# A two-layer metaformer step on one Trainium2 core: all five engine orders rewritten, FFN pixels turned by DMA, moments on VectorE

## The chip, the cores and the metric

One NeuronCore of a Trainium2 chip. The metric is the device time of one launch in microseconds, as the median of several executions. The kernel drives five engines with their own instruction streams: TensorE (PE), VectorE (DVE), ScalarE (ACT), GpSimd (POOL) and SyncE (SP, which only issues DMAs). They meet in semaphores alone.

## What is computed

`x` has the shape (16, 96, 96, 96): 16 images, 96 channels, 96 x 96 pixels. Two layers follow one another; every token is one pixel with its 96 channels.

```
# layer 0
x = x + conv0(_ln_c(x))                 # patches of 3x3, see below
t = t + ffn(_ln_t(t))                   # 96 -> 384 -> relu -> 96, operands rounded to e5m2, sums to fp16
# conv0, for each 3x3 patch (9 pixels):
y       = patches . w_mask / (x_norm * w_norm)       # cosine with 512 vectors, 9 pixels each
idx     = argmax over 512 x 9 ; max_ch, max_col = idx // 9, idx % 9
inp     = [max_act * max_sim + w_mask[max_ch] * (1 - max_sim), y[max_ch, :]]
out     = 1x1 conv of l2(relu(l1(tanh(i2(leaky_relu(i1(inp)))))))
# layer 1
x = x + n / (2 + 1e-4 * box5x5(sum_c n^2)) ** 0.75   # n = _ln_c(x)
t = t + ffn(_ln_t(t))
```

## The kernel before

**Tiles.** A tile is 128 patches of 9 pixels (`J` = 9), so 128 partitions x 9 x 96 values; an image has 8 tiles (`SLOTS`), the input 128 (`NT`). `x_tok` holds a tile with tokens on the partitions, `x_chan` with channels on them.

**Steps.** One software-pipelined loop, `steps(body)`, runs on each engine over k from -4 on. In step k each stage works on another tile, by the offsets in `PARTS`: `fs` (k+4, statistics of the input), `f1` (k+3, scores), `f2` (k+2, the picked vector), `f3` (k+1, the MLP and conv), `back` (k, hidden part of the first FFN `ffn0`), `tail` (k-1, its output), `root2` (k-2, sums for LRN), `columns` and `pre` (k-10, k-11, LRN applied and layer-1 normalisation), `rear` (k-12, hidden part of `ffn1`) and `rtail` (k-13, its output and the store). Within a step, the order of the work is written out by hand in the `body` of each engine, and each engine does its instructions in that order. Once per image come `window_parts` and `window_sums` (step 1 of 8: the 5 x 5 box as 15 shift matmuls) and `lrn_columns` (step 2 of 8: the polynomial and a root, some 25 instructions on VectorE).

**Stages that the change touches.**
- `score` (L383) multiplies a pixel with the 512 vectors, one fp32 matmul into one of two banks, and waits in `score_taken` for VectorE's `score_max` (L742) of two scores before. `win_scores` (L401) puts the picked pixel's scores into the same banks; the score behind it waits for `vidx_ready` from `win_vector` (L783).
- `select` (L750) on VectorE finds the best pixel of a patch; three instructions with an accumulator (L771 to L776) pick its mean, its reciprocal deviation and its best score. `gather_pixel` and `gather` on GpSimd fetch rows by indirect DMA; `dot_product` on GpSimd multiplies them with the nine pixels.
- `mlp_input` (L791) on VectorE builds `inp` (the last instruction is L807). The MLP goes back and forth: `mlp_turn` (L407), `mlp_in`, `mlp_mid`, `mlp_last`, `conv` on TensorE with ScalarE's copies `inpT`, `h`, `vcs`, `h1` between, and `residual1` (L810) on VectorE at its end.
- Statistics: `group_stats` (L736) runs `bn_stats` over 9 pixels for three tiles (input, `x1`, `x2`); `moments` (L947) on GpSimd turns them into means, sums of squares and arguments of roots with nine chained instructions; `pixel_roots` (L721) on VectorE takes the roots at the start of the next step (`args_ready`, then `root_ready`). GpSimd's `body` waits for `root_ready` before anything else.
- Both FFNs pass through two PSUM banks each in 14 units a tile (`UNITS`): 3 units turn the fp8 pixels (L363: transposes by matmul with an identity; ScalarE copies them to `xT`), 9 make the hidden values (L370, 384 columns each), 2 the output (L378). `fill` on TensorE and `take` on ScalarE alternate over `filled` and `taken`; VectorE adds the bias, applies relu and rounds to e5m2 (`hidden`, L820: L825 three times, L833 once).
- `ffn_output` (L989) on GpSimd adds bias and residual in two passes per FFN.
- SyncE loads `xt` and `xc` of tile `fs` (`load_tokens`, `load_pixels`), then stores the tile `rtail`.

## Time and profile before

| | before |
|---|---|
| median of 3 runs | 3559.91 us (3558.04 to 3561.16) |
| the profiled execution | 3554.84 us, its span 3553.0 us |
| busy PE / DVE / ACT / POOL | 3011.0 / 2778.1 / 2832.7 / 2566.0 us |
| mean granted TensorE clock | 0.958 of full |
| HBM read / written | 134.72 / 57.02 MB |

A row of the profile's page or of the trace gives times in us from the start of the span, durations in us (ns where marked), and the line of the kernel. A row with xN stands for N instructions of a kind that follow one another. An instruction's duration includes its passage through the engine's pipeline, so the next one of the same engine may start before it ends; a busy time is the union of such durations. In square brackets stands how long the engine was idle ahead of the instruction, and for whom.

### The profile page before, as it was taken

To read this page: it belongs to the slowest core of one execution; us is meant where nothing else is said; L and a number is where in the kernel's file an instruction comes from. 1 tells how busy PE (TensorE), PEld (TensorE's weight loads), DVE (VectorE), ACT (ScalarE), POOL (GpSimd) and SP (SyncE) were. 2 spreads that over 40 slices of the span, in tenths; PEclk is the share of its full clock that TensorE was granted. 3 is DMA by queue.
4 is the path that set the end of the run, shared out by engine and by line. 5 is a ranking of instruction groups with operands and counts; after the bars stand their busy time and mean duration, and the time that the engine had idled before them with its cause. 6 is when DMAs were issued, how large, how long until landed. Compare 5 with 4: busy or idle time off the path is not lost. (4 is left out here: it accounts for less than half of the span.)

```text
span 3553.0 us, 62660 instructions
## 1 busy us (share of the span) xinstructions
PE 3011.0 (85%) x18190; PEld 1688.2 (48%) x18190; DVE 2778.1 (78%) x10043; ACT 2832.7 (80%) x7303; POOL 2566.0 (72%) x3993
## 2 busy tenths in 40 slices
PE   5888888888888888888888888888888888888755
PEld 2444454454545445445544545454444555445432
DVE  6777888888888888888888888888888888888631
ACT  0444788888888888888888888888878888888977
POOL 2455787777778777777877777787777778777753
PEclk9999999999999999999999999999999999999855
DMA  3111121211112121111212111121212112121000
GB/s 88 38 45 47 45 63 52 65 54 57 61 57 62 52 67 51 57 61 56 62 52 67 52 58 60 57 62 52 66 51 64 55 57 62 52 66 42 24 31 35
DMA packets 64607, 195.78 MB, mean 55 GB/s; under 512 B 11394, under 2 KB 14732, under 8 KB 64268
## 3 DMA queue, kind: packets, MB, share of 16 engines
q1 hardware_dynamic: 54028, 172.89, 15.1%
q0 software_dynamic: 10240, 18.89, 2.1%
q8 instruction: 150, 2.46, 0.3%
q14 instruction: 189, 1.55, 0.1%
HBM read 134.72 MB, written 57.02 MB: 54 GB/s over the span
## 5 line engine op out<-in xcount | busy, mean ns | idle before, releaser
L527 ACT ACTIVATE ffn_hid<-banks 128x384 f16<-128x384 f32 x2304 | 1026.8, 487 | 260.0 <-PE banks L370 236.7
L393 PE MATMUL banks<-wcT,xc 128*128 128x512 f32 x2304 | 1187.8, 618 | 50.2 <-DVE mx L745 43.4
L745 DVE TENSOR_REDUCE mx<-banks 128x1 f32<-128x512 f32 x1152 | 781.4, 687 | 428.8 <-PE banks L393 427.6
L370 PE MATMUL banks<-ffn_xT,w1q 128*128 128x384 bf16 x2304 | 668.8, 343 | 177.3 <-ACT ffn_hid L527 138.0
L994 POOL TENSOR_TENSOR ffn_f<-ffn_y,b2q 128x864 f16<-128x864 f16 x256 | 465.3, 1818 | 288.3 <-DVE nb L731 209.7
L370 PEld LDWEIGHTS banks<-ffn_xT,w1q 128*128 128x128 bf16 x2304 | 226.1, 98 | 775.8 <-ACT ffn_hid L527 589.4
L393 PEld LDWEIGHTS banks<-wcT,xc 128*128 128x128 f32 x2304 | 414.5, 196 | 282.8 <-issue 140.8
L825 DVE TENSOR_SCALAR ffn_hid<-ffn_hid,b1q 128x1152 f16<-128x1152 f16 x768 | 405.8, 551 | 139.0 <-ACT ffn_hid L527 138.6
L996 POOL TENSOR_TENSOR x<-x,ffn_f 128x864 f32<-128x864 f32 x256 | 466.6, 1823 | 20.1
L560 ACT ACTIVATE ffn_x<-x,cols 128x96 fp8e5<-128x96 f32 x1152 | 461.3, 456 | 0.0
L560 ACT ACTIVATE ffn_x<-x,nb,roots 128x96 fp8e5<-128x96 f32 x1152 | 425.1, 456 | 0.0
L738 DVE BATCH_NORM_STATS2 st<-x 128x6 f32<-128x96 f32 x2304 | 406.0, 245 | 13.1 <-POOL x L996 13.1
L984 POOL TENSOR_TENSOR prod_dot<-xt,wrow 128x864 f32<-128x864 f32 x128 | 263.3, 2057 | 195.4 <-DMA wrow<-vector_table,vidx 195.4
L437 PE MATMUL banks<-wc,h 128*128 128x480 f32 (+1 forms) x1024 | 393.8, 528 | 0.0
L527 ACT ACTIVATE ffn_xT<-banks 96x384 bf16<-96x384 f32 x768 | 345.0, 484 | 57.0 <-PE banks L363 37.1
L378 PEld LDWEIGHTS banks<-w2q,ffn_hid 128*128 128x128 f16 x6912 | 335.0, 100 | 116.6 <-issue 115.1
L527 ACT ACTIVATE ffn_y<-banks 128x480 f16<-128x480 f32 (+1 forms) x512 | 256.8, 531 | 161.3 <-PE banks L378 144.7
L378 PE MATMUL banks<-w2q,ffn_hid 128*128 128x96 bf16 x6912 | 351.3, 210 | 37.1 <-DVE ffn_hid L833 37.1
L363 PE MATMUL banks<-ident_b,ffn_x 128*96 128x128 bf16 x2304 | 227.6, 227 | 146.9 <-ACT ffn_xT L527 118.8
L363 PEld LDWEIGHTS banks<-ident_b,ffn_x 128*96 128x96 fp8e5 x2304 | 175.8, 125 | 257.1 <-ACT ffn_xT L527 157.2
L573 ACT ACTIVATE x<-x,cols 128x96 f32<-128x96 f32 x640 | 293.5, 461 | 0.2 <-POOL cols L1004 0.2
L833 DVE TENSOR_SCALAR ffn_hid<-ffn_hid 128x3456 uint16<-128x3456 uint16 x256 | 270.5, 1057 | 4.0
(153 smaller groups left out, 4178.6 us busy)
## 6 DMA issues: line engine op xcount, KB each, us to landing
xt<-x_tok_in SPq DMA_DIRECT2D x128, 432.0 KB, 3.2
xc<-x_chan_in SPq DMA_DIRECT2D x128, 432.0 KB, 3.6
out_tok<-x SPq DMA_DIRECT2D x128, 432.0 KB
win<-x_tok_in,xrow POOLq DMA_INDIRECT x128, 2.6
wrow<-vector_table,vidx POOLq DMA_INDIRECT x128, 2.9
shift<-shift_in SPq DMA_DIRECT2D x1, 960.0 KB
vector_table<-wtab SPq DMA_DIRECT2D x1, 384.0 KB, 2.9
w1raw<-w_in SPq DMA_DIRECT2D x1, 288.0 KB
```

Of the source, the lines that this page charges most:

```text
L363: last = pe.matmul(bank[0:C, i * P:(i + 1) * P], ffn.x8[:, u * G + i, :], ident_b[:, :], start=True, stop=True)
L370: last = pe.matmul(bank[:, 0:GW], w1q[:, ffn.layer, c * P:(c + 1) * P], ffn.xT[:, g * GW:(g + 1) * GW], start=True, stop=True)
L378: last = pe.matmul(bank[:, (j - j0) * C:(j - j0 + 1) * C], ffn.hid[:, c, j * P:(j + 1) * P], w2q[:, ffn.layer, c, :], start=(c == 0), stop ...
L393: last = pe.matmul(ps_score[score_bank(j)], xc[p][:, j, :], wcT[:, :], start=True, stop=True)
L437: last = pe.matmul(bank[:, 0:(j1 - j0) * C], h1[:, q, :], wc[:, q, j0 * C:j1 * C], start=(q == 0), stop=(q == 1))
L527: return nc.scalar.activation(dst, src, ACT.Copy)
L560: last = nc.scalar.activation(ffn.x8[:, j, :], x[:, j, :], ACT.Identity, bias=bias_c[:, j:j + 1], scale=scale_c[:, j:j + 1], saturate=False)
L738: last = nc.vector.bn_stats(st3[:, which, j, :], src[:, j, :])
L745: nc.vector.tensor_reduce(mx[p][:, j:j + 1], ps_score[score_bank(j)], AX.X, ALU.max).then_inc(score_taken, 1)
L825: nc.vector.tensor_scalar(ffn.hid[:, c, :], ffn.hid[:, c, :], b1q[:, ffn.layer, c:c + 1], 0.0, ALU.add, ALU.max).then_inc(ffn.rounded, 1)
L994: tt(ffn.f[:, :, :], ffn.y[:, :, :], b2, ALU.add).then_inc(ffn.f_ready, 1)
L996: tt(dst, x, ffn.f[:, :, :], ALU.add).then_inc(ready, 1)
```

## The change

Only the order and place of work change, and two steps of how it is done:

- The fp8 pixels of each FFN are no longer turned on TensorE. ScalarE writes them in pairs (`x8` [P, 5, 128, 2]: two pixels' bytes side by side), SyncE issues one `dma_start_transpose` for each FFN and tile over 5 x 128 two-byte elements of 128 partitions, and the hidden matmuls read `xT` with a step of two bytes, in pieces of 512, 512 and 128 columns. `UNITS` becomes 11.
- `moments` moves from GpSimd to VectorE: seven instructions, woven with `select` at the end of the step. The three accumulating picks become one product and one reduction over `pix`, in which twice the mean, sum of squares and roots lie together; a third `mix` instruction halves the mean.
- `keep_root2` becomes one copy, `tile_columns` one; the squares for LRN are made once per image (two instructions more in `window_parts`).
- GpSimd no longer waits for `root_ready` at the head of its step; its order is bias of `ffn1`, bias and sum of `ffn0`, LRN rest, `gather`, `keep_root2`, `window_parts`, `dot_product`, `tile_columns`, `gather_pixel`, and the sum of `ffn1` last.
- SyncE turns both FFNs' pixels, then loads for the next step, then stores.
- The bodies of TensorE, ScalarE and VectorE are ordered anew, as below.

```diff
-UNITS = G + HC * G + 2
+COLUMNS = [(0, 512), (512, 1024), (1024, J * P)]
+UNITS = HC * G + 2
@@ sync
+            def turn(ffn, tile):
+                sp.wait_ge(ffn.x8_ready, tile + 1)
+                wait_past(sp, ffn.filled, tile * UNITS - 2)
+                sp.dma_start_transpose(ffn.xT[:, :, :], ffn.x8[:].rearrange("p a c t -> p (a c t)").bitcast(F16)
+                                       ).then_inc(ffn.turned, 16)
             def body(k):
+                if k.back is not None:
+                    turn(ffn0, k.back)
+                if k.pre is not None:
+                    turn(ffn1, k.pre)
+                load(Step(k.k + 1))
                 if k.rtail is not None:
                     sp.wait_ge(x4_ready, k.rtail + 1)
                     sp.dma_start(out[k.rtail], x4[k.q][:]).then_inc(x4_stored[k.q], 16)
@@ tensor, fill
-                    if u < G:
...
-                        for i in range(J // G):
-                            last = pe.matmul(bank[0:C, i * P:(i + 1) * P], ffn.x8[:, u * G + i, :],
-                                             ident_b[:, :], start=True, stop=True)
+                    if u < HC * G:
+                        c, g = divmod(u, G)
                         if u == 0:
-                            pe.wait_ge(ffn.x8_ready, tile + 1)
+                            pe.wait_ge(ffn.turned, (tile + 1) * 16)
+                        c0, c1 = COLUMNS[g]
+                        pairs = ffn.xT[:, c0 // (2 * P):(c1 + P) // (2 * P), :].bitcast(F8).rearrange(
+                            "p a (x t) -> p a t x", t=2)
...
+                        last = pe.matmul(bank[:, 0:c1 - c0], w1q[:, ffn.layer, c * P:(c + 1) * P], pairs,
+                                         start=True, stop=True)
@@ tensor, body
                 scores(0, 2)
-                if k.tail is not None:
-                    fill(ffn0, k.tail, G + HC * G, 2)
+                hidden_units(ffn1, k.rear, 0, 2)
+                out_units(ffn0, k.tail, k.tail_p, 0)
+                out_units(ffn0, k.tail, k.tail_p, 1)
+                hidden_units(ffn1, k.rear, 2, 2)
+                scores(2, 3)
                 if k.f3 is not None:
                     mlp_turn(k.f3)
-                if k.rear is not None:
-                    fill(ffn1, k.rear, 0, G)
+                hidden_units(ffn1, k.rear, 4, 1)
+                if k.f2 is not None:
+                    win_turn(k.f2, k.q)
...
                 if k.f3 is not None:
                     mlp_in(k.f3)
+                hidden_units(ffn1, k.rear, 5, 1)
+                scores(3, WIN_TURN)
                 if k.f2 is not None:
+                    win_scores(k.f1, k.f2)
...
                     mlp_mid(k.f3)
+                scores(WIN_TURN, 5)
+                hidden_units(ffn1, k.rear, 6, 2)
+                scores(5, 6)
                 if k.f3 is not None:
                     mlp_last(k.f3)
+                scores(6, 7)
+                hidden_units(ffn1, k.rear, 8, 1)
                 if k.f3 is not None:
                     conv(k.f3)
-                if k.back is not None:
-                    fill(ffn0, k.back, 0, G)
                 hidden_units(ffn0, k.back, 0, 2)
                 scores(7, 8)
                 hidden_units(ffn0, k.back, 2, 2)
+                scores(8, J)
                 window_sums(k, 0, 5)
-                scores(8, J)
                 hidden_units(ffn0, k.back, 4, 2)
                 window_sums(k, 5, 10)
+                out_units(ffn1, k.rear, k.rear_p, 0)
+                out_units(ffn1, k.rear, k.rear_p, 1)
                 hidden_units(ffn0, k.back, 6, 3)
@@ scalar, body (norm0: nine pixels of ffn0, behind root_ready; norm1: of ffn1)
+                take_hidden(ffn1, k.rear, 5, 1)
+                norm0(k, 0, 3)
+                lrn_pixels(k, 4, XA)
+                norm0(k, 3, 5)
                 ... vcs ...
+                norm0(k, 5, J)
+                take_hidden(ffn1, k.rear, 6, 1)
                 ... h1 ...
+                take_hidden(ffn1, k.rear, 7, 2)
+                norm1(k, 0, XA)
+                norm1(k, XA, XA + 1)
+                take_hidden(ffn0, k.back, 0, 2)
+                norm1(k, XA + 1, XA + 2)
+                take_hidden(ffn0, k.back, 2, 2)
+                norm1(k, XA + 2, J)
+                take_hidden(ffn0, k.back, 4, 2)
+                take_out(ffn1, k.rear, k.rear_p)
+                take_hidden(ffn0, k.back, 6, 3)
@@ vector
+            def moments(tile, p):
+                dve.wait_ge(stats_ready, tile + 1)
+                wait_past(dve, root_ready, tile)
+                wait_past(dve, kept, tile - 6)
...
@@ vector, body
+                    mlp_input(k.f3, k.p, roots_of, lambda: scores(0, 1))
+                run(roots_of, 3)
+                scores(1, 2)
+                run(roots_of, 2)
+                scores(2, 3)
+                run(roots_of)
+                scores(3, WIN_TURN, factors, 2)
+                relu(ffn1, k.rear, 0)
+                    last = group_stats(1, xt[:, k.fs & XT - 1], 0, 6, factors)
+                    win_vector(k.f2, k.q, factors)
+                    last = group_stats(1, xt[:, k.fs & XT - 1], 6, J, factors)
+                scores(WIN_TURN, 5, factors, 2)
+                relu(ffn1, k.rear, 1)
+                    last = group_stats(2, x2[:, k.tail & RING - 1], 0, 6, factors)
+                scores(5, 7, factors, 2)
+                relu(ffn1, k.rear, 2)
+                    last = group_stats(2, x2[:, k.tail & RING - 1], 6, J, factors)
+                run(factors)
+                round_up(ffn1, k.rear)
                     residual1(k.f3, k.q)
                 scores(7, 8)
+                    last = group_stats(0, x1[k.q], 0, J, iter(()))
                 scores(8, J)
+                for c in range(HC):
+                    for _ in range(2):
+                        run(moments_of, 1)
+                        run(select_of, 1)
...
+                    relu(ffn0, k.back, c)
+                round_up(ffn0, k.back)
@@ gpsimd, body
-                if k.moments is not None:
-                    pool.wait_ge(root_ready, k.moments + 1)
+                if k.rtail is not None:
+                    ffn_bias(ffn1, k.rtail, x4_ready)
                 if k.tail is not None:
+                    ffn_bias(ffn0, k.tail, x2_ready)
                     ffn_output(ffn0, k.tail, x1[k.q][:, :, :], x2[:, k.tail & RING - 1], x2_ready)
...
-                if k.stats is not None:
-                    moments(k.stats, k.q)
                 if k.f1 is not None:
                     gather_pixel(k.f1, k.p)
+                if k.rtail is not None:
+                    pool.wait_ge(x4_stored[k.q], landed(k.rtail, k.q))
+                    ffn_output(ffn1, k.rtail, x3[:, k.rtail3], x4[k.q][:, :, :], x4_ready)
```

## Rows read from the trace of the kernel before

**Rows 1.** The profile's page, head: busy us, share of the span, instructions
```profile
span 3553.0 us, 62660 instructions
PE 3011.0 (85%) x18190; PEld 1688.2 (48%) x18190; DVE 2778.1 (78%) x10043; ACT 2832.7 (80%) x7303; POOL 2566.0 (72%) x3993
```

**Rows 2.** One line's instructions (L803): ns min/median/max, first and last start us
```profile
L803 DVE TENSOR_SCALAR wnorm<-win,wmean,mix x128: 318/329/422, 64.3 to 3326.9; 128x96 f32<-128x96 f32 x128
```

**Rows 3.** Stretches between store issues, and the end: from:to, length, busy by engine
```profile
1759.84:1786.80 26.96, 24.39 (x166) 15.53 (x167) 20.41 (x76) 21.66 (x57) 23.57 (x44) 1.00 0.18 56
1786.80:1816.99 30.19, 24.55 (x141) 13.12 (x139) 27.10 (x97) 22.55 (x59) 19.49 (x30) 0.94 0.15 50
1816.99:1841.86 24.87, 22.18 (x138) 12.39 (x138) 20.59 (x76) 22.04 (x58) 19.46 (x30) 1.00 0.19 60
3326.86:3553.00 226.14, 127.75 (x795) 71.93 (x791) 71.19 (x163) 170.71 (x434) 112.11 (x179) 0.57 0.08 30
```
(The engines stand in the order PE, PE's weight loads, DVE, ACT, POOL; then TensorE's granted clock, the DMA engines' busy share and GB/s.)

**Rows 4.** Timeline of VectorE in a plain step: start us, us, instruction [idle before]
```profile
1836.17 0.69 DVE L745 TENSOR_REDUCE mx<-banks 128x1 f32<-128x512 f32 x1 [0.62 <-PE banks L393]
...
1849.97 0.69 DVE L745 TENSOR_REDUCE mx<-banks 128x1 f32<-128x512 f32 x1 [1.17 <-PE banks L393]
...
1855.24 0.19 DVE L765 TENSOR_TENSOR xrow<-jidx,row_base 128x1 uint32<-128x1 uint32 x1
1855.36 0.16 DVE L767 TENSOR_TENSOR pick<-iota,jidx 128x9 f32<-128x9 f32 x1
1855.55 0.20 DVE L771 SCALAR_TENSOR_TENSOR junk<-pick,mom 128x9 f32<-128x9 f32 x1
...
1855.87 0.59 DVE L798 TENSOR_REDUCE dots<-half_dot 128x9 f32<-128x432 f32 x1
...
1857.22 0.31 DVE L807 SCALAR_TENSOR_TENSOR inp<-wrow,mix,wnorm 128x96 f32<-128x96 f32 x1
...
1858.14 0.20 DVE L718 SCALAR_TENSOR_TENSOR roots<-rtmp,roots 128x36 f32<-128x36 f32 x1
1858.37 0.20 DVE L708 SCALAR_TENSOR_TENSOR rtmp<-roots 128x36 f32<-128x36 f32 x1
```

**Rows 5.** Timeline of TensorE in the same step
```profile
1832.73 0.32 PE L410 MATMUL banks<-ident,inp 128*106 128x128 f32 x1 [0.39 <-DVE inp L807]
1832.88 0.50 PE L363 MATMUL banks<-ident_b,ffn_x 128*96 128x128 bf16 x6
...
1834.01 0.85 PE L415 MATMUL banks<-inpT,wi 106*96 106x128 f32 x6
...
1845.17 1.88 PE L393 MATMUL banks<-wcT,xc 128*128 128x512 f32 x4
1846.89 0.50 PE L363 MATMUL banks<-ident_b,ffn_x 128*96 128x128 bf16 x6
...
1857.59 0.32 PE L410 MATMUL banks<-ident,inp 128*106 128x128 f32 x1 [0.38 <-DVE inp L807]
```

**Rows 6.** Waits from 1500 to 2400 us: who for whom, us, times, longest
```profile
DVE mx L745 <- PE banks L393: 110.7, 205, 1.3
...
PE banks L363 <- ACT ffn_xT L527: 33.1, 70, 1.0
```

**Rows 7.** Timeline of GpSimd in the same step: first and last of `moments`
```profile
1852.19 0.49 POOL L955 TENSOR_TENSOR mtmp<-st 128x27 f32<-128x27 f32 x2 [1.04 <-DVE st L738]
...
1856.26 0.25 POOL L962 TENSOR_TENSOR args<-var,eps 128x27 f32<-128x27 f32 x1
```

**Rows 8.** Timeline of ScalarE in the same step: three copies of turned pixels
```profile
1833.28 1.42 ACT L527 ACTIVATE ffn_xT<-banks 96x384 bf16<-96x384 f32 x3
```

**Rows 9.** The page's DMA issues: KB each, median us from issue to landing
```profile
xt<-x_tok_in SPq DMA_DIRECT2D x128, 432.0 KB, 3.2
...
wrow<-vector_table,vidx POOLq DMA_INDIRECT x128, 2.9
```

More of the change, by code:

```diff
@@ L20 @@
 from contextlib import ExitStack
+from itertools import chain
 import numpy as np
@@ L158, in build @@
         pow_half = sb("pow_half", [P, V // P])
-        half, c24, inv_c = (sb(n, [P, 3, J]) for n in ("half", "quarter_c", "inverse_c"))
         eps = sb("eps", [P, 3, J])
@@ L590, in take_hidden, with take_out @@
                     if tile is not None:
-                        take(ffn, tile, G + first, units)
-                if k.tail is not None:
-                    take(ffn0, k.tail, G + HC * G, 2)
-                lrn_pixels(k, 0, 1)
+                        take(ffn, tile, k.back_p if ffn is ffn0 else k.rear_p, first, units)
+                def take_out(ffn, tile, parity):
+                    if tile is not None:
+                        take(ffn, tile, parity, HC * G, 2)
+                take_hidden(ffn1, k.rear, 0, 1)
+                lrn_pixels(k, 0, 1)
+                take_hidden(ffn1, k.rear, 1, 1)
+                lrn_pixels(k, 1, 2)
+                take_out(ffn0, k.tail, k.tail_p)
+                take_hidden(ffn1, k.rear, 2, 2)
+                lrn_pixels(k, 2, 3)
                 if k.f3 is not None:
@@ L661, in _ @@
             nc.vector.memset(wc[:], 0.0)
-            for operand in (*xc, wcT, winT, w1q, ffn0.xT, ffn1.xT):
+            for ffn in (ffn0, ffn1):
+                nc.vector.memset(ffn.x8[:].rearrange("p a c t -> p (a c t)").bitcast(U16), 0)
+            for operand in (*xc, wcT, winT, w1q):
                 last = nc.vector.memset(operand[C:P], 0.0)
@@ L889, in body, with scores @@
             def body(k):
-                between = pixel_roots(k) if k.moments is not None else iter(())
-                def scores(j0, j1, links=0):
+                roots_of = pixel_roots(k) if k.moments is not None else iter(())
+                factors = lrn_columns(k.lrn, k.pre) if k.lrn is not None else iter(())
+                last = None
+                def scores(j0, j1, between=iter(()), links=0):
                     for j in range(j0, j1):
@@ L927, in body @@
                 scores(8, J)
-                between = select(k.f1, k.p) if k.f1 is not None else iter(())
-                if k.back is not None:
-                    hidden(ffn0, k.back, between)
-                run(between)
+                select_of = select(k.f1, k.p) if k.f1 is not None else iter(())
+                moments_of = moments(k.stats, k.q) if k.stats is not None else iter(())
+                for c in range(HC):
+                    for _ in range(2):
+                        run(moments_of, 1)
+                        run(select_of, 1)
+                    if c == HC - 1:
+                        run(moments_of)
+                        run(select_of)
+                    relu(ffn0, k.back, c)
+                round_up(ffn0, k.back)
             steps(body)
```

322 lines of the change are left out of this document (141 added, 181 removed).

## The prediction

> **What bounds the kernel now.** The head of the page comes first: TensorE is busy 85% of the span, ScalarE 80%, VectorE 78%, GpSimd 72% [rows 1]. None is full, so the order of work between them counts. The step is regular: the `wnorm` instruction of line 803 runs 128 times from 64.3 to 3326.9 us, so a step takes 25.69 us on average [rows 2]. Cut from store issue to store issue there are three kinds: 24.87 us for a plain step, 26.96 us for the one with the window sums, 30.19 us for the one with the LRN polynomial, each of the last two once in eight [rows 3]. Those eight make 6 x 24.87 + 26.96 + 30.19 = 206.4 us. By busy time the plain step has 22.18 us of TensorE, 20.59 of VectorE, 22.04 of ScalarE and 19.46 of GpSimd; the LRN step has 27.10 of VectorE [rows 3].
>
> The loop that closes the step is read from two timelines. TensorE starts `mlp_turn` (L410) right behind VectorE's `inp` (L807) at 1832.73, works through both transposes, the MLP and seven scores, and gives score 7, for which VectorE has waited 1.17 us at 1849.97 [rows 4, 5]. From there VectorE works without a wait to L807 at 1857.22, and TensorE, idle since its last projection, starts the next L410 at 1857.59. That is 17.2 us on TensorE and 7.6 us on VectorE. In this half TensorE runs nine fp8 transposes twice and is held by ScalarE's copies of them. The waits agree: over 35 steps the transposes wait 33.1 us for `ffn_xT`, and VectorE 110.7 us for scores [rows 6]. GpSimd closes no loop: its last moments instruction, at 1856.26, is done before VectorE comes to the root chain [rows 7].
>
> **Part 1, pixels turned by DMA.** It removes 18 transposes from TensorE and 6 copies from ScalarE in each step. On TensorE the first block runs from 1832.88 to the next work at 1834.01, 1.1 us, and the second, from 1846.89 on, is its like with 0.2 us of waits more, so 2.4 us in all [rows 5]; on ScalarE 6 copies, 3 of them in 1.42 us, give 2.7 us [rows 8]. The hidden matmuls keep 1152 columns in 9 pieces (512, 512, 128 in place of 3 x 384), so I cost that at zero, between -0.3 and +0.5 us a step; the cover is two scores or pixels beside each pair. That the moving operand now steps over two bytes has no row here: from nothing to 2.9 us of TensorE (18 hidden matmuls of 384 columns of 0.16 us each, once more), and I take nothing: even the upper end would go into the slack that TensorE has below.
>
> The added thing is the latency of two DMAs of 160 KB a step. No row shows such a DMA. The nearest are the 432 KB token load, 3.2 us to landing, and the gathers, 2.9 us [rows 9]. I take 3.5 us, with 2.9 and 8 us as the ends. The cover for `ffn0`: its normalised pixels are ready some 9.5 us behind the start of VectorE's step, and its first hidden unit is wanted at 13.5; the loss begins at about 4.5 us of latency and grows one for one. For `ffn1` pixels end at about 16 and are wanted at 19.5 to 22, a cover of 5 us or so. The queue of SyncE carries them ahead of the next loads and behind the store of the step before. The load of tile k+5 is then issued near 16.5 us and used a step later, which hides it; the store now waits for GpSimd's last sum, and must be issued before 9.5 us of the next step, which it is by some 8 us.
>
> The Trainium skill (Advanced Engine Details and Errata, X-Bar Transpose) says that a transposing DMA on this chip is about as fast as a plain one, at 350 to 400 GB/s. By it the 160 KB would add under 0.5 us to a gather's 2.9 us, an estimate of 3.4 us, and the DMA would be hidden. No row here shows one.
>
> **Part 2, moments on VectorE.** GpSimd's chain from 1852.19 to 1856.5 goes, 4.3 us a step [rows 7], and with five copies fewer GpSimd keeps about 14.7 of its 19.46 busy us. VectorE gains seven 27-element instructions. A dependent one of 36 elements has a pitch of 0.23 us in the root chain (1858.14 to 1858.37), neighbours without a dependency 0.12 us (1855.24 to 1855.36) [rows 4]. Woven into `select` they lie between: I take 0.15 us, 1.05 us in all, ends 0.8 and 1.6. Three accumulating picks (1855.55 to the next work at 1855.87, 0.32 us) become a product and a reduce (0.35), and one more `mix` costs 0.12. The sum is +1.2 us.
>
> The Trainium skill (VectorE: DVE Perf Modes, The DRAIN you can't avoid) speaks against this part: the pipe empties behind each VectorE instruction, with or without a semaphore, so the count of instructions is what costs. This case's trace agrees for the dependent pitch of 0.23 us and not for the 0.12 us of neighbours.
>
> **Part 3, the new order.** VectorE takes score 0 inside `mlp_input`, and TensorE calls `mlp_turn` after score 2, with four hidden units and the output projection ahead of it. From L410 to score 7 I count on TensorE by start-to-start time: five scores of 0.86 (two run from 1845.17 to 1846.89 [rows 5]), 4.3; the window score 0.86; the MLP's three matmul groups 2.1; conv 2.9 (up to 1845.17); hidden units 1.2 and two turns 0.5. That makes 11.8 us against 17.2. VectorE's half grows from 7.6 to 9.4 us (moments 1.2, score 0 at 0.6). The two are 21.2 us, and four handovers of 0.2 to 0.4 us (L807 to L410 is 0.37) bring them to about 22.4: as much as VectorE's own work, below.
>
> **The step after.** VectorE now: 24.87 less its seven waits of the sample step (0.62 at 1836.17 the first, 1.17 at 1849.97 the last, 3.91 in all) is 20.96 us [rows 4]. With +1.2 it is 22.2 us, the floor of the plain step. TensorE's sum by pitch is 19.2 us (ten scores 8.6, conv 2.9, MLP and turns 2.5, hidden 2.9, projections 2.3), ScalarE's 22.04 - 2.7 = 19.3, GpSimd's 14.7. What is late next is VectorE itself, then two tight handovers: `vidx` ahead of score 5 and score 7 behind conv, each within 0.4 us by my count. I add 0.6 us for such waits: 22.8 us. The window step keeps its +2.0 (15 shift matmuls in TensorE's slack, but GpSimd's window parts also end just in time): 24.8. The LRN step is already VectorE's own, 27.10 us busy of 30.19 [rows 3]; it becomes 27.1 + 1.2 and about 1.1 of gaps, 29.4. Eight steps: 6 x 22.8 + 24.8 + 29.4 = 191.0, so 15.4 us less, times 127/8 = 245 us.
>
> **Ends.** Set-up gains some memsets and a first turn, +2 us. From 3326.86 to the end, 226 us, there are thirteen shorter steps without a score, in which ScalarE's takes, VectorE's rounding and the projection follow one another, with TensorE's mean granted clock at 0.57, so mostly at its lower level of 1.2 GHz [rows 3]. There the DMA is not covered; the transposes, their copies and one wait (some 3 us) leave and 3.5 us comes, +5 us over the last 11 steps. Sum: span 3553.0, time of the profiled run 3554.8; 3554.8 - 245 + 7 = 3317. The median is 5.1 us above the profiled run, which gives 3322; I say 3320.
>
> **Rivals.**
> (A) The forecast, VectorE-bound at 22.2 to 23.6 us: 3240 to 3430 us, 57%.
> (B) The coupling keeps some of it: in-order ScalarE has `norm0` (nine pixels behind the root chain) ahead of `vcs` and `h1`, so conv comes late, and the step settles at 24.0 us. For it: today's loop holds over 2 us of waits on TensorE though none looks long. Price 1.2 x 127 = 152 us, so about 3470 us; 21%.
> (C) Each small VectorE instruction costs its full chain pitch of 0.23 us, ten of them 2.3 in place of 1.2 us: +1.1 x 127, some 3460 us; for it the root chain's even 0.23, against it the 0.12 pairs; 8%, inside the range of B. The rule on the pipe in the Trainium skill (VectorE: DVE Perf Modes, The DRAIN you can't avoid) is this rival.
> (D) The turning DMA is late, on the other side. It decides from 4.5 us of latency, and equals today's time at about 6.6 us (24.87 - 22.8 = 2.1 above 4.5). At 8 us each step is 3.5 longer, +445 us, and the drain +50: 3815 us. For it: it moves 81 920 elements of two bytes, where the rows below 3.6 us move whole runs of one partition, and nothing bounds its rate; against it: 432 KB land in 3.2 us, nearly three times its bytes. 12%, of which 10 are above 6.6 us and slower than before.
> (E) The change does nothing for the time, because ScalarE (22.04 busy) was the real bound and only its 2.7 us count against longer takes: within 0.2% of before, 2%.
>
> **Numbers.** Measurements here can tell about 0.2% from no change. Faster: A, B, C and 2 in 100 for a late DMA below 6.6 us, 0.88; same 0.02 (E); slower 0.10. The range 3235 to 3490 holds A, B and C but for their tails; it leaves out D and some of E.
>
> **What would show it.** Plain steps of 22.8 us between stores; VectorE idle under 1 us a step; no wait of TensorE for `ffn_xT`; landing of the turned pixels at 3 to 4.5 us; GpSimd near 63% busy. The prediction is wrong if hidden matmuls wait for the DMA (D), if VectorE still waits over 1.5 us a step for scores or for conv (B), or if the moments take over 1.6 us (C).

## The result, and the profile after

| | before | after |
|---|---|---|
| median | 3558.97 us | 4008.78 us |
| ratio | 1 | 1.127 (1.1244 to 1.1288) |
| profiled execution, its span | 3554.84, 3553.0 us | 4007.11, 4005.3 us |
| VectorE, GpSimd busy | 78%, 72% | 94%, 51% |

The change makes the kernel 12.7% slower; 3320 us was forecast, within 3235 to 3490. One of the four executions of the changed kernel took 4324.45 us at a mean granted clock of 0.639 (0.893 in the profiled one) and is not in the ratio.

The head of the page of the changed kernel answers to [rows 1], the row of `wnorm` (now L870; min, median and max ns, first and last start) to [rows 2]:

```profile
span 4005.3 us, 55754 instructions
PE 2981.2 (74%) x15886; PEld 1626.2 (41%) x15886; DVE 3770.5 (94%) x10587; ACT 2459.5 (61%) x6535; POOL 2047.7 (51%) x1799
...
L870 DVE TENSOR_SCALAR wnorm<-win,mix x128: 315/317/326, 66.0 to 3802.8; 128x96 f32<-128x96 f32 x128
```

A mean step takes (3802.8 - 66.0) / 127 = 29.42 us against 25.69. Stretches of the changed kernel between store issues, as in [rows 3] (the window step, the LRN step, a plain one, and all that follows the last `wnorm`; engines in the order PE, PE's weight loads, VectorE, ScalarE, GpSimd; then granted clock, DMA share, GB/s):

```profile
1726.32:1755.66 29.34, 23.66 (x147) 15.19 (x148) 28.11 (x80) 17.54 (x47) 19.79 (x28) 0.94 0.22 62
1755.66:1788.59 32.93, 24.04 (x125) 11.79 (x123) 32.59 (x102) 21.13 (x55) 15.50 (x12) 0.95 0.19 56
1818.43:1848.25 29.82, 21.70 (x120) 12.09 (x120) 29.55 (x80) 19.04 (x51) 15.61 (x12) 0.94 0.21 62
3802.83:4005.30 202.47, 106.35 (x651) 57.40 (x649) 89.24 (x184) 147.64 (x380) 94.00 (x93) 0.57 0.15 46
```

VectorE works 29.55 of the 29.82 us of a plain step, so it is the bound, as forecast, yet with about as many instructions as before (80 against 76) it is busy 9 us longer. TensorE, ScalarE and GpSimd have all become lighter. TensorE's granted clock is lower (0.94 of full in the plain step, 1.00 in the kernel before), but that isn't the cause: VectorE waits 26 us for scores in the whole run, where it waited 428. What grew is found by grouping VectorE's instructions by line and shape (count | busy us, mean ns | idle before). First the kernel before, then the changed one; L718 became L752, L708 L742, L711 L745, L715 L749, L825 (relu) L891 and L833 (rounding) L899:

```profile
L745 DVE TENSOR_REDUCE mx<-banks 128x1 f32<-128x512 f32 x1152 | 781.4, 687 | 428.8 <-PE banks L393 427.6
L825 DVE TENSOR_SCALAR ffn_hid<-ffn_hid,b1q 128x1152 f16<-128x1152 f16 x768 | 405.8, 551 | 139.0 <-ACT ffn_hid L527 138.6
L833 DVE TENSOR_SCALAR ffn_hid<-ffn_hid 128x3456 uint16<-128x3456 uint16 x256 | 270.5, 1057 | 4.0
L711 DVE TENSOR_TENSOR rtmp<-rtmp,args 128x36 f32<-128x36 f32 x266 | 52.1, 196 | 9.1
L718 DVE SCALAR_TENSOR_TENSOR roots<-rtmp,roots 128x36 f32<-128x36 f32 x266 | 52.0, 196 | 9.1
L708 DVE SCALAR_TENSOR_TENSOR rtmp<-roots 128x36 f32<-128x36 f32 x266 | 51.4, 193 | 4.8
L715 DVE SCALAR_TENSOR_TENSOR rtmp<-rtmp 128x36 f32<-128x36 f32 x133 | 26.0, 196 | 4.5
```

```profile
L812 DVE TENSOR_REDUCE pix<-banks 128x1 f32<-128x512 f32 x1152 | 770.0, 677 | 26.3 <-PE banks L417 26.0
L891 DVE TENSOR_SCALAR ffn_hid<-ffn_hid,b1q 128x1152 f16<-128x1152 f16 x768 | 761.6, 992 | 104.0 <-ACT ffn_hid L552 104.0
L899 DVE TENSOR_SCALAR ffn_hid<-ffn_hid 128x3456 uint16<-128x3456 uint16 x256 | 483.9, 1890 | 4.8
L752 DVE SCALAR_TENSOR_TENSOR pix<-rtmp,pix 128x36 f32<-128x36 f32 x266 | 259.2, 974 | 4.8
L742 DVE SCALAR_TENSOR_TENSOR rtmp<-pix 128x36 f32<-128x36 f32 x266 | 237.2, 892 | 4.7
L745 DVE TENSOR_TENSOR rtmp<-rtmp,args 128x36 f32<-128x36 f32 x266 | 100.8, 379 | 4.8
L749 DVE SCALAR_TENSOR_TENSOR rtmp<-rtmp 128x36 f32<-128x36 f32 x133 | 56.6, 425 | 4.5
```

The score reduction, which reads PSUM, is unchanged (687 and 677 ns). Relu went from 551 to 992 ns on the same 1152 elements, rounding from 1057 to 1890, the root chain's instructions on 36 elements from some 195 to 974, 892, 379 and 425. Per step (six relus, two roundings, seven root instructions) that is 6 x 0.441 + 2 x 0.833 + 2 x (0.778 + 0.699 + 0.183) + 0.229 = 7.9 us. The forecast's floor of 22.2 and 7.9 make 30.1, and the plain step takes 29.8.

Where the time sits is seen in the timeline of a plain step of the changed kernel: VectorE and then GpSimd over the same stretches (start, duration, instruction):

```profile
1844.98 0.51 DVE L891 TENSOR_SCALAR ffn_hid<-ffn_hid,b1q 128x1152 f16<-128x1152 f16 x1
...
1845.89 2.66 DVE L891 TENSOR_SCALAR ffn_hid<-ffn_hid,b1q 128x1152 f16<-128x1152 f16 x1
1848.58 2.55 DVE L899 TENSOR_SCALAR ffn_hid<-ffn_hid 128x3456 uint16<-128x3456 uint16 x1
...
1853.39 0.20 DVE L745 TENSOR_TENSOR rtmp<-rtmp,args 128x36 f32<-128x36 f32 x1
...
1854.33 1.74 DVE L752 SCALAR_TENSOR_TENSOR pix<-rtmp,pix 128x36 f32<-128x36 f32 x1
1856.11 1.87 DVE L742 SCALAR_TENSOR_TENSOR rtmp<-pix 128x36 f32<-128x36 f32 x1
```

```profile
1845.26 1.12 POOL L1030 DMA_INDIRECT win<-x_tok_in,xrow  x1 [5.27 <-DVE xrow L832]
1846.39 1.83 POOL L1061 TENSOR_TENSOR x<-x,ffn_f 128x864 f32<-128x864 f32 x1
1848.37 1.85 POOL L1056 TENSOR_TENSOR ffn_f<-ffn_y,b2q 128x864 f16<-128x864 f16 x1
1854.21 1.81 POOL L1056 TENSOR_TENSOR ffn_f<-ffn_y,b2q 128x864 f16<-128x864 f16 x1 [3.99 <-ACT ffn_y L552]
1856.10 1.82 POOL L1061 TENSOR_TENSOR x<-x,ffn_f 128x864 f32<-128x864 f32 x1
```

One relu takes 0.51 us, its like 0.9 us later 2.66, ending 0.3 us behind GpSimd's add. A root instruction takes 0.20 us while GpSimd is idle and 1.74 and 1.87 us when GpSimd's adds of 864 elements (L1056, L1061) start just before it. In the kernel before the same adds stood here (its timeline, GpSimd first, then VectorE):

```profile
1834.44 1.82 POOL L994 TENSOR_TENSOR ffn_f<-ffn_y,b2q 128x864 f16<-128x864 f16 x1 [1.43 <-DVE nb L731]
1836.33 1.82 POOL L996 TENSOR_TENSOR x<-x,ffn_f 128x864 f32<-128x864 f32 x1
```

```profile
1834.27 1.28 DVE L745 TENSOR_REDUCE mx<-banks 128x1 f32<-128x512 f32 x2
1836.17 0.69 DVE L745 TENSOR_REDUCE mx<-banks 128x1 f32<-128x512 f32 x1 [0.62 <-PE banks L393]
1837.97 1.53 DVE L738 BATCH_NORM_STATS2 st<-xt 128x6 f32<-128x96 f32 x9
```

They fall on score reductions and statistics, at their usual durations. Over the whole run, the 465 us of L994 overlap VectorE for 234 us in L738, 166 us in L745 and some 1 us in a relu; the 472 us of L1056 overlap it for 182 us in the rounding, 28 in relu and 211 in the root chain, and the 468 us of L1061 for 222 us in relu and 225 in the root chain. GpSimd's wait for `root_ready`, which the change takes away, starts them behind the root chain (runs 1 and 2 test this).

The turned pixels are no trouble. The page's DMA issues (answers to [rows 9]; count, median us to landing) and the waits of the whole run (total, times, longest):

```profile
ffn_xT<-ffn_x SPq DMA_TRANSPOSE x256, 2.6
```

```profile
PE banks L394 <- DMA ffn_xT<-ffn_x: 18.4, 12, 1.9
```

### The profile page after: what moved, and what is told of

It reads as the page before. It is cut to its first block, busy times and chain, and to the rows that moved or that the text cites. A ratio compares the mean times of both kernels' runs of the same rounds, so it can differ in the third digit from the quotient of the medians.

```text
span 4005.3 us, 55754 instructions
## 1 busy us (share of the span) xinstructions
PE 2981.2 (74%) x15886; PEld 1626.2 (41%) x15886; DVE 3770.5 (94%) x10587; ACT 2459.5 (61%) x6535; POOL 2047.7 (51%) x1799
## 4 chain that ended last, share of the span: by engine, by line
DVE 70%; issue 13%; PE 6%; POOL 4%; ACT 3%; DMA 3%; SPq 0%; POOLq 0%; DVEq 0%
DVE ffn_hid L891 15%; DVE st L803 11%; DVE pix L812 11%; DVE pix L752 6%; DVE rtmp L742 5%; DVE ffn_hid L899 4%; DVE x L882 3%; DVE rtmp L745 2%; DVE vidx L852 2%; PE banks L417 2%; DVE dots L862 2%; DMA win<-x_tok_in,xrow 1%; ACT ffn_hid L552 1%; DVE rtmp L749 1%; PE banks L462 1%
## 5 line engine op out<-in xcount | busy, mean ns | idle before, releaser
L552 ACT ACTIVATE ffn_hid<-banks 128x512 f16<-128x512 f32 (+1 forms) x2304 | 1032.4, 490 | 382.0 <-PE banks L394 381.2
L402 PE MATMUL banks<-w2q,ffn_hid 128*128 128x96 bf16 x6912 | 447.2, 238 | 614.2 <-DVE ffn_hid L899 614.2
L891 DVE TENSOR_SCALAR ffn_hid<-ffn_hid,b1q 128x1152 f16<-128x1152 f16 x768 | 761.6, 992 | 104.0 <-ACT ffn_hid L552 104.0
L394 PE MATMUL banks<-ffn_xT,w1q 128*128 128x512 fp8e5 (+1 forms) x2304 | 688.5, 355 | 148.4 <-ACT ffn_hid L552 123.1
L812 DVE TENSOR_REDUCE pix<-banks 128x1 f32<-128x512 f32 x1152 | 770.0, 677 | 26.3 <-PE banks L417 26.0
L1056 POOL TENSOR_TENSOR ffn_f<-ffn_y,b2q 128x864 f16<-128x864 f16 x256 | 471.7, 1843 | 589.5 <-ACT ffn_y L552 572.8
L585 ACT ACTIVATE ffn_x<-x,nb,pix 128x96 fp8e5<-128x96 f32 x1152 | 450.5, 458 | 291.0 <-DVE nb L765 291.0
L899 DVE TENSOR_SCALAR ffn_hid<-ffn_hid 128x3456 uint16<-128x3456 uint16 x256 | 483.9, 1890 | 4.8
L1061 POOL TENSOR_TENSOR x<-x,ffn_f 128x864 f32<-128x864 f32 x256 | 468.4, 1830 | 11.9
L1030 POOL DMA_INDIRECT win<-x_tok_in,xrow x128 | 143.1, 1118 | 621.6 <-DVE xrow L832 621.6
L803 DVE BATCH_NORM_STATS2 st<-x 128x6 f32<-128x96 f32 x2304 | 407.5, 239 | 0.1
L1038 POOL DMA_INDIRECT wrow<-vector_table,vidx x128 | 126.4, 988 | 475.2 <-DVE vidx L852 465.6
L752 DVE SCALAR_TENSOR_TENSOR pix<-rtmp,pix 128x36 f32<-128x36 f32 x266 | 259.2, 974 | 4.8
```

Source lines behind the costliest of these rows:

```text
L394: last = pe.matmul(bank[:, 0:c1 - c0], w1q[:, ffn.layer, c * P:(c + 1) * P], pairs, start=True, stop=True)
L402: last = pe.matmul(bank[:, (j - j0) * C:(j - j0 + 1) * C], ffn.hid[:, c, j * P:(j + 1) * P], w2q[:, ffn.layer, c, :], start=(c == 0), stop ...
L552: return nc.scalar.activation(dst, src, ACT.Copy)
L585: last = nc.scalar.activation(ffn.x8[:, j // 2, 0:C, j % 2], x[:, j, :], ACT.Identity, bias=bias_c[:, j:j + 1], scale=scale_c[:, j:j + 1], ...
L752: chain.add(stt(out=y, in0=t, scalar=float(outer), in1=y, op0=ALU.add, op1=ALU.mult))
L803: last = nc.vector.bn_stats(st3[:, which, j, :], src[:, j, :])
```

## The experiments

The theory to be tested (P): while a long GpSimd instruction on SBUF runs, a VectorE instruction with two SBUF inputs, or a fast fp16 one, waits for its end, and this, not the DMA turning (D) and not the new order of the other engines or its latencies (L), makes the kernel slow. Ratios are to the kernel before on the same chip, with 95% intervals.

**1. The wait of GpSimd put back, in the changed kernel.**

```diff
@@ gpsimd, body
+                if k.moments is not None:
+                    pool.wait_ge(root_ready, k.moments + 1)
                 if k.rtail is not None:
                     ffn_bias(ffn1, k.rtail, x4_ready)
```

> The changed kernel with one wait put back: GpSimd waits for root_ready at the head of each step. Theory P (one at a time): a VectorE instruction with two SBUF inputs, and the fp16 relu and rounding, cannot run beside a GpSimd elementwise instruction; each waits out the one that runs. Then the root chain (973 and 892 ns an instruction in the changed kernel, 196 before) comes back to about 200 ns, worth up to 3.5 us a step, and part of it is lost again to the relus of ffn1 that GpSimd's four adds then meet: 3700 to 3950 us. Theory D (the turning DMAs slow VectorE's SBUF access) and theory L (roots, means and sums now lie together in one tile, and reading them there is slow): the root chain stays at 900 ns, and the added wait can only cost, 4010 us or more.

Measured: 3821.97 us, 1.073 (1.0714 to 1.075), a mean step of 27.95 us. Two groups of VectorE:

```profile
L891 DVE TENSOR_SCALAR ffn_hid<-ffn_hid,b1q 128x1152 f16<-128x1152 f16 x768 | 859.1, 1119 | 94.9 <-ACT ffn_hid L552 94.9
L752 DVE SCALAR_TENSOR_TENSOR pix<-rtmp,pix 128x36 f32<-128x36 f32 x266 | 50.6, 190 | 4.9
```

The root chain is back at 190 ns with nothing changed on VectorE, and 187 us are regained; rounding fell to 1508 ns, but the adds moved onto relus, now 1119 ns. So the root chain's part is the missing wait's, and the rest is where in VectorE's new order GpSimd's work falls.

**2. The wait taken away, in the kernel before.** Nothing of the new order, no DMA turning.

```diff
@@ gpsimd, body
-                if k.moments is not None:
-                    pool.wait_ge(root_ready, k.moments + 1)
                 if k.tail is not None:
```

> The kernel before with one wait taken away: GpSimd's wait for root_ready at the head of the step. Nothing else changes, no DMA turns and no tile moves. Theory P: GpSimd's first two adds of 1.82 us now run beside the root chain; its instructions go from 196 ns to 500 ns and more, and as VectorE's stretch closes the loop each step grows by 1 to 3 us, so 3690 to 3940 us. Theories D and L: the wait was idle time of an engine with room, 3559 us within 0.3%, root chain at 196 ns.

Measured: 4653.7 us, 1.306 (1.3043 to 1.3086); a mean step of 34.34 us. VectorE's groups, and the largest wait of GpSimd in the run:

```profile
L711 DVE TENSOR_TENSOR rtmp<-rtmp,args 128x36 f32<-128x36 f32 x266 | 302.5, 1137 | 9.2
L718 DVE SCALAR_TENSOR_TENSOR roots<-rtmp,roots 128x36 f32<-128x36 f32 x266 | 253.0, 951 | 9.1
L708 DVE SCALAR_TENSOR_TENSOR rtmp<-roots 128x36 f32<-128x36 f32 x266 | 240.9, 906 | 4.9
L715 DVE SCALAR_TENSOR_TENSOR rtmp<-rtmp 128x36 f32<-128x36 f32 x133 | 184.2, 1385 | 4.6
```

```profile
POOL wrow L976 <- DVE vidx L788: 1035.7, 112, 10.8
```

One wait removed costs 1091 us (against 3562.6 us of the kernel before beside it). The direction is P's, and L and D are out as its cause; the size is far above my figure. The root chain alone has grown by 799 us (981 against 182), relu and rounding (706 and 1309 ns) by 184 us together; in the kernel before the chain opens VectorE's step and the scores stand behind it, so it is on the path. The profiled spans differ by 1100 us (4653.2 against 3553.0): VectorE is busy 1018 us more, 983 of them in these groups, and idle 82 us more, in longer waits for scores (475 us against 428) and for the picked pixel's scores (132 against 97).

**3. The adds made short, in the changed kernel.** The four adds of a step work on one channel of 96 (their place, waits and number stay), so most of both FFNs' bias and sum is left out. Some memsets in set-up cost 13 us of VectorE's time.

```diff
-                tt(ffn.f[:, :, :], ffn.y[:, :, :], b2, ALU.add).then_inc(ffn.f_ready, 1)
+                tt(ffn.f[:, :, 0:1], ffn.y[:, :, 0:1], b2[:, :, 0:1], ALU.add).then_inc(ffn.f_ready, 1)
...
-                tt(dst, x, ffn.f[:, :, :], ALU.add).then_inc(ready, 1)
+                tt(dst[:, :, 0:1], x[:, :, 0:1], ffn.f[:, :, 0:1], ALU.add).then_inc(ready, 1)
```

> The changed kernel with GpSimd's two bias adds and two residual adds in each step cut from 96 channels to one (work left out: output and second-layer inputs are wrong in the other channels; x2 and x4 are filled once at the start, some 16 us). All turning DMAs, the moments on VectorE and all orders stay. Theory P: relu 992 to about 560 ns, rounding 1890 to about 1100, root chain 974 and 892 to about 250; the step becomes what I predicted for the change, 22.5 to 23.5 us, and the time 3330 to 3470 us. Theories D and L: those durations and about 4000 us stay.

Measured: 3302.84 us, 0.927 (0.9257 to 0.9288), with a mean step of 23.87 us. Relu 703, rounding 1238, the longest root instruction 346 ns. The time is below the 3330 to 3470 us that I expected, and the durations are above the 560, 1100 and 250 ns. The same order and the same DMAs, 706 us less: everything that went wrong hangs on how long these four instructions run. What remains above 551 and 1057 ns is beside the dot product (90 relus of 1836 ns each beside L1049 and L1051).

**4. The adds made short, in the kernel before.** The same cut, as the counter-test.

> The kernel before with GpSimd's four long adds cut to one channel, as in e3_short_adds (work left out; x2 and x4 filled once, some 16 us). It tells what GpSimd's adds cost the kernel before. Theory P with an order that keeps them apart: under 2% is gained, 3500 to 3575 us, as against 18% for the changed kernel. If the adds cost VectorE as much there, the time falls below 3400 us.

Measured: 3591.88 us, 1.010 (1.0079 to 1.0113), a mean step of 25.95 us. I had expected a small gain. The long adds lie beside instructions that don't wait for them; with short ones GpSimd's dot product comes earlier and falls on VectorE's relus, of which 82 now take 2272 ns. Relu and rounding take 178 us more than before (700 and 1304 ns a piece), yet the time grows by 34 us only, and VectorE waits 286 us for scores in place of 428. So this run doesn't show that the adds cost nothing here: a gain from less GpSimd work may lie hidden under the new collisions. It shows that the cut gives nothing where it doesn't take collisions away. In the changed kernel (run 3) it takes 791 us off relu, rounding and root chain, more than the 706 us by which the time falls. Where the long instructions fall decides.

**5. Only the writes kept.** As 3, with a memset of 128 x 800 fp32 on GpSimd ahead of each shortened add: an instruction that writes SBUF and reads nothing.

```diff
+                nc.gpsimd.memset(dump[:, ffn.layer], 0.0)
                 tt(ffn.f[:, :, 0:1], ffn.y[:, :, 0:1], b2[:, :, 0:1], ALU.add).then_inc(ffn.f_ready, 1)
...
+                nc.gpsimd.memset(dump[:, 2 + ffn.layer], 0.0)
                 tt(dst[:, :, 0:1], x[:, :, 0:1], ffn.f[:, :, 0:1], ALU.add).then_inc(ready, 1)
```

> As e3_short_adds (GpSimd's four long adds cut to one channel, work left out), with a GpSimd memset of 128x800 fp32 set ahead of each of the four: GpSimd is busy at the same places but reads nothing from SBUF there. If what VectorE waits for is GpSimd's reading, two-input instructions (root chain) stay near the 244 to 346 ns of e3_short_adds, and the time stays near 3300 us unless relu and rounding still wait for a writer. If being busy is enough (any GpSimd instruction, or its semaphores), the root chain goes back to 500 ns and more and the time to 3450 us and above.

Measured: 3445.46 us, 0.968 (0.9662 to 0.9701). VectorE's relu and the root chain, and the memsets:

```profile
L895 DVE TENSOR_SCALAR ffn_hid<-ffn_hid,b1q 128x1152 f16<-128x1152 f16 x768 | 629.7, 820 | 123.6 <-ACT ffn_hid L553 123.4
L756 DVE SCALAR_TENSOR_TENSOR pix<-rtmp,pix 128x36 f32<-128x36 f32 x266 | 94.7, 356 | 4.8
```

```profile
L1060 POOL MEMSET dump<- 128x800 f32 x256 | 289.2, 1130 | 372.9 <-ACT ffn_y L553 359.4
L1066 POOL MEMSET dump<- 128x800 f32 x256 | 198.3, 775 | 7.8
```

The means mix cases, so I sorted each line's instructions by the GpSimd instructions that they overlap:

| VectorE instruction | beside | count | mean ns |
|---|---|---|---|
| root L756, two inputs | nothing | 70 | 202 |
| the same | a memset (L1060 or L1066) alone | 97 | 184 |
| the same | L1086, which reads | 75 | 774 |
| relu L895, one fp16 input | nothing | 295 | 508 |
| the same | the gather L1034 (and a wait) | 111 | 513 |
| the same | L1034, the memset L1066 and the shortened add L1067 | 97 | 1584 |
| relu L894 of run 3 | the gather and the shortened add, no memset | 98 | 738 |

Two kinds come apart. The two-input instruction waits for a GpSimd instruction that reads SBUF and passes one that only writes. The fp16 `TENSOR_SCALAR` waits for a writer too: 1584 ns with the memset, 738 without it. It goes the other way as well: rounding beside L1060 keeps 1060 ns (111 of them), and the memset L1060 beside it takes 1.6 us (110 of them), while all but one of the others of that line take 765 to 787 ns. Nor does it take 16-bit elements: in run 4 a `TENSOR_SCALAR` with one fp32 input of 72 elements (L866, once an image) takes 1819 ns on average beside the dot product (14 of 16) and 188 ns beside nothing.

**6. GpSimd in the order of the kernel before, in the changed kernel.** Head wait, bias and sum of `ffn0`, bias and sum of `ffn1`, then the rest.

```diff
@@ gpsimd, body
-                if k.rtail is not None:
-                    ffn_bias(ffn1, k.rtail, x4_ready)
+                if k.moments is not None:
+                    pool.wait_ge(root_ready, k.moments + 1)
...
+                if k.rtail is not None:
+                    ffn_bias(ffn1, k.rtail, x4_ready)
+                    pool.wait_ge(x4_stored[k.q], landed(k.rtail, k.q))
+                    ffn_output(ffn1, k.rtail, x3[:, k.rtail3], x4[k.q][:, :, :], x4_ready)
```

> The changed kernel with GpSimd in the order of the kernel before (wait for root_ready, both passes of ffn0, both passes of ffn1, LRN rest, gather, and so on), the moments still on VectorE. Theory P: the root chain at 200 ns, the relus and rounding of ffn0 at the end of the step at 550 and 1050 ns, as GpSimd is idle there, and the relus of ffn1, which now stand singly inside GpSimd's 9 us of adds, at 1000 to 2000 ns: 3600 to 3850 us. Theories D and L: all stay slow, 4000 us or more.

Measured: 3614.02 us, 1.014 (1.0121 to 1.0159): 395 us of the loss come back from GpSimd's body alone. Plain steps now take 24.7 us, as before the change; relus are still 789 ns, since VectorE's new order scatters three of them over scores, statistics and adds.

**7. VectorE's blocked kinds gathered.** As 6, with the root chain in one piece and the three relus of `ffn1` together behind score 6.

```diff
@@ vector, body
-                run(roots_of, 3)
-                scores(1, 2)
-                run(roots_of, 2)
-                scores(2, 3)
                 run(roots_of)
+                scores(1, 3)
...
                 run(factors)
+                relu(ffn1, k.rear, 0)
+                relu(ffn1, k.rear, 1)
+                relu(ffn1, k.rear, 2)
                 round_up(ffn1, k.rear)
```

> The kernel of e4_pool_order (GpSimd in its old order) with VectorE's order mended: the root chain runs in one piece, so that GpSimd starts sooner, and the three relus of ffn1 stand together behind score 6, where GpSimd's adds are nearly over. The moments stay on VectorE. Theory P: relu mean down from 789 to 600 to 700 ns, window step down from 32.2 us as GpSimd starts 1.2 us sooner, plain step 24.0 to 24.8 us: 3480 to 3580 us. A rival, that placement inside VectorE's order does not matter since the blocked time only moves from one instruction to another: 3600 us within 0.5%.

Measured: 3466.11 us, 0.973 (0.9712 to 0.9754). Relu 680, rounding 1117 ns, plain steps of 23.4 us, so better than expected. With GpSimd's body the same as in run 6, the place in VectorE's order alone is worth 148 us.

**8. The moments back on GpSimd.** As 7, with the chain of `moments` on GpSimd between `tile_columns` and `gather_pixel`.

```diff
@@ vector, body
-                moments_of = moments(k.stats, k.q) if k.stats is not None else iter(())
@@ gpsimd, body
+                if k.stats is not None:
+                    moments(k.stats, k.q)
                 if k.f1 is not None:
                     gather_pixel(k.f1, k.p)
```

> As e5_grouped, with the moments chain back on GpSimd (behind tile_columns, ahead of gather_pixel), so VectorE loses seven small instructions; turned pixels and TensorE's and ScalarE's new orders stay. If VectorE's instruction count is what is left of the loop, 1.1 us a step come off e5_grouped, 3340 to 3440 us. If GpSimd's chain, which shares with the relus of ffn0, costs more than it saves, no gain against e5_grouped or a loss: 3500 us or more.

Measured: 3407.04 us, 0.957 (0.9548 to 0.9598). The move is worth 23.39 - 22.82 = 0.57 us of the median step, 59 us in all. That is net of what GpSimd's chain costs VectorE at its new place: beside it two instructions of `select` go from 179 to 340 ns (`sim`) and from 162 to 383 ns (`pick`). So this part of the change costs, in this order, rather than gains.

**9. The once-per-image work moved.** As 8. Window steps took 30.5 us and LRN steps 31.5 there; the window sums go to the end of TensorE's step, the polynomial's pieces behind `mlp_input` and among the relus, and `keep_root2` behind `dot_product` in the other steps.

```diff
@@ tensor, body
-                window_sums(k, 0, 5)
                 hidden_units(ffn0, k.back, 4, 2)
-                window_sums(k, 5, 10)
...
-                window_sums(k, 10, WINDOW_PARTS)
+                window_sums(k, 0, WINDOW_PARTS)
@@ vector, body
-                run(factors, 1)
...
+                run(factors, 1)
                 run(roots_of)
...
-                scores(WIN_TURN, 5, factors, 2)
+                scores(WIN_TURN, 5)
...
+                for c in range(HC):
+                    relu(ffn1, k.rear, c)
+                    run(factors, 1)
```

> As e6_pool_moments, with the work that comes once an image moved: all 15 window matmuls behind ffn0's last hidden units (in e6_pool_moments they stand ahead of them, and TensorE waits 3.67 us for GpSimd's window parts with ScalarE and VectorE queued behind it), the LRN factors on VectorE only behind the picked vector's index (in e6_pool_moments TensorE waits 5.01 us for it in the LRN step), keep_root2 behind dot_product. If those two waits make the 30.8 and 31.5 us steps, they become about 26 and 29 us and the time 3290 to 3350 us; if the two steps are long because VectorE and GpSimd simply have that much work in them, 3390 us or more.

Measured: 3333.49 us, 0.937 (0.9357 to 0.9388), 6.3% below the kernel before and 16.8% below the changed one, with the whole computation in it. Plain steps take 22.8 us, window steps 26.3, LRN steps 30. Its two VectorE groups:

```profile
L861 DVE TENSOR_SCALAR ffn_hid<-ffn_hid,b1q 128x1152 f16<-128x1152 f16 x768 | 481.5, 648 | 95.0 <-ACT ffn_hid L551 94.9
L869 DVE TENSOR_SCALAR ffn_hid<-ffn_hid 128x3456 uint16<-128x3456 uint16 x256 | 293.1, 1145 | 8.3
```

All kernels by mean and median step (`wnorm` to `wnorm`, us):

| kernel | mean | median | us |
|---|---|---|---|
| before | 25.69 | 24.87 | 3559 |
| before, short adds (4) | 25.95 | 25.46 | 3592 |
| before, no wait (2) | 34.34 | 35.25 | 4654 |
| changed | 29.42 | 29.82 | 4009 |
| changed, wait put back (1) | 27.95 | 28.38 | 3822 |
| changed, short adds (3) | 23.87 | 23.27 | 3303 |
| short adds and memsets (5) | 24.97 | 25.27 | 3445 |
| GpSimd's old order (6) | 26.28 | 24.77 | 3614 |
| and VectorE gathered (7) | 25.12 | 23.39 | 3466 |
| and moments on GpSimd (8) | 24.61 | 22.82 | 3407 |
| and once-per-image moved (9) | 24.07 | 22.88 | 3333 |

## Why the prediction was wrong

**The step that failed** is the one named "The step after". It took VectorE's 20.96 us of work from the trace of before and set it, as it was, into a new order: every relu at 0.5 us, every root instruction at 0.20. These durations held because GpSimd's long instructions lay beside score reductions and statistics. Beside the adds the same instructions take 2.66, 2.55, 1.74 and 1.87 us, and in a mean step 7.9 us are added, a term that the sum doesn't have. Of the 690 us between forecast (3317 us for the profiled run) and the profiled 4007, longer steps are +719: 127 steps took 3736.8 us where 3262.6 - 245 = 3017.6 were forecast. The ends are -29: 66.0 + 202.5 us outside the steps, where 64.3 + 226.1 + 7 were.

**The second failure is the sentence "GpSimd closes no loop".** The prediction took the end of GpSimd's moments for all that GpSimd has to do with the step, and gave its order no price in any rival. Its wait at the head of the step kept the adds off the root chain; run 2 shows it to be worth 1091 us in the kernel before. The engines don't meet in semaphores alone, as the description of the chip has it: VectorE and GpSimd also hold each other up where no semaphore stands between them.

**What the trace of before already showed.** The reading that was missed is one of the same kind of instruction at two durations, with the other engine beside it. The LRN step of the kernel before has one, first VectorE, then GpSimd:

```profile
1791.87 2.27 DVE L825 TENSOR_SCALAR ffn_hid<-ffn_hid,b1q 128x1152 f16<-128x1152 f16 x1
1794.06 1.13 DVE L708 SCALAR_TENSOR_TENSOR lbuf<-cols_i 128x72 f32<-128x72 f32 x1
1795.11 0.51 DVE L825 TENSOR_SCALAR ffn_hid<-ffn_hid,b1q 128x1152 f16<-128x1152 f16 x1
```

```profile
1791.37 2.45 POOL L984 TENSOR_TENSOR prod_dot<-xt,wrow 128x864 f32<-128x864 f32 x1 [1.73 <-DMA wrow<-vector_table,vidx]
1793.89 1.20 POOL L986 TENSOR_TENSOR half_dot<-prod_dot 128x432 f32<-128x432 f32 x1
```

One relu took 2.27 us beside the dot product's first instruction and the next 0.51 with GpSimd past it; 72 elements of the root took 1.13 us beside the second. The other direction stood in the very stretch that the prediction quoted in part, GpSimd's moments [rows 7]:

```profile
1854.38 1.04 POOL L958 TENSOR_TENSOR mtmp<-mtmp,quarter_c 128x27 f32<-128x27 f32 x1
1855.50 0.23 POOL L959 TENSOR_TENSOR ss<-mtmp 128x27 f32<-128x27 f32 x1
```

Both work on 27 elements; the one of 1.04 us ran beside a rounding (1854.29, 1.03 us). Over the run, L958 takes 243 ns with nothing of VectorE beside it (10 of them) and 1035 beside a rounding (98).

The Trainium skill (SBUF — State Buffer, Who interferes with whom) states the rule: VectorE and GpSimd share one pair of SBUF ports as an exclusive lock, held for the whole instruction, which a VectorE instruction wants if it has two SBUF inputs and GpSimd reads, or if it runs in a two-port mode, as `tensor_scalar` can; reductions never do. The runs agree in these points: 184 against 774 ns for the two-input instruction beside a writer and a reader, 1584 against 738 ns for relu with and without a writer, and in the kernel before 692 ns for the score reduction beside the add L996 and 685 beside nothing. That it is a two-port mode which makes relu wait, no run here shows. This rule speaks against the change and should have been its main rival.

**Point by point.**
- Pixels turned by DMA: right. 3.5 us of latency was taken, 2.6 us is the median, and TensorE waits 18.4 us in the whole run. Rival D (late DMA) is out: run 3 has the same DMAs and takes 3303 us. The gain of ScalarE is there too: 19.04 us busy in a plain step, 19.3 forecast.
- Hidden matmuls over a step of two bytes, costed at nothing: not separated from the rest. TensorE's busy time in the plain step is 21.70 us for 120 instructions, and it isn't the bound.
- Moments on VectorE: +1.2 us forecast, 1.05 of them for the seven instructions. In the changed kernel, from the start of each of the seven to the start of VectorE's next, it is 74 to 117 ns by the median, 0.74 us together (0.93 by the means). The sign is right, the size somewhat too large, and rival C (0.23 us each) is out. The 0.57 us between runs 7 and 8 are net of collisions and don't measure this term. The product and reduction for the picks take 177 and 181 ns.
- VectorE as the bound, idle under 1 us a step: right (29.55 of 29.82 us).
- The new order without the collision: right in size, but in part by luck. Run 3 has mean steps of 23.87 us, where 191.0 / 8 = 23.9 was forecast, and 3303 us against 3320. Yet it leaves most of the adds out, and by the growth of relu, rounding and root chain over the kernel before it still holds 1.8 us of collisions a step, which the forecast doesn't have. The moments term, 0.1 to 0.3 us too large, made up for some of it; the rest isn't traced. Plain steps there take 23.2 or some 24.7 us, so how much is coupling (B, 24.0 us) and how much a collision that is left isn't told apart; run 9 comes to 22.8 us, with the moments on GpSimd.
- GpSimd's load: 14.7 us forecast for a plain step, 15.61 measured; its 2048 us are 62% of a span of 3317 and only 51% of this one.
- LRN and window step: 29.4 and 24.8 forecast, 27.6 and 23.4 to 24.8 in run 3; 32.9 and 29.3 in the changed kernel.
- The ends: +7 forecast, -22 measured (268.5 against 290.4 us outside the steps). Where in the step `wnorm` stands also moved, so the figure is rough.

**Open.** By which record of the trace the winner of such a collision can be told: the relu at 1845.89 starts 0.5 us ahead of the add at 1846.39 and yet ends behind it, with the gather L1030 between them, and the 97 relus of 1584 ns in run 5 look the same. By what property of a `TENSOR_SCALAR` it waits for a writer (its type, its length, where its operands lie) wasn't tested.

## What to carry to other kernels

A duration from a trace holds for the neighbour that the instruction had there. Before the order between VectorE and GpSimd is changed, list which VectorE instructions have two SBUF inputs or are `tensor_scalar`s from SBUF to SBUF (fp16 and uint16 here, and one in fp32), which long GpSimd instructions there are, and lay the ones beside PSUM readers, reductions and statistics, by a wait if need be: a wait at the head of a body can be worth more than the idle time that it shows. When the same line and shape shows two durations, look at what the other engine does at that moment before anything is summed.

## What the runs showed of the hardware that was not expected

- A two-input VectorE instruction on 36 elements, 0.19 us by itself, takes up to 1.87 us beside a GpSimd add on 864 elements of 1.82 us. In the kernel before, taking away the wait that keeps a chain of seven such instructions off four adds costs 30.6% of the whole time; 799 of the 1091 us are the chain's own durations (run 2).
- A GpSimd memset, which reads nothing, leaves such an instruction at 184 ns and stretches an fp16 relu from 738 ns, beside a gather and a short add, to 1584 (runs 3 and 5).
- A GpSimd gather by indirect DMA (1.12 us) hardly disturbs relu: 513 ns beside it in run 5 (111 of them) and 515 in the kernel before (199), against 508 and 515 beside nothing.
- A VectorE `TENSOR_SCALAR` on 72 fp32 elements, one input, 188 ns by itself, takes 1819 ns on average beside GpSimd's product of 864 elements (run 4).
- A transposing DMA of 160 KB from SBUF to SBUF lands in 2.6 us (median of 256).
